# Values of two pairs turned by DMA, the first pair's weights doubled across the partitions, its context loaded from ScalarE's queue, and the last output in halves

## What is computed

```python
def _autocorrelation(Q, K, V):          # H = 8 heads, C = 2, L = 64
    ...
    corr = jnp.fft.ifft(qf * jnp.conj(kf), axis=2).real
    topk = int(C * np.log(L))           # 8
    w, idx = jax.lax.top_k(corr.transpose(0, 1, 3, 2), topk)
    w = jax.nn.softmax(w, axis=-1)
    for i in range(topk):
        g = jnp.minimum(idx[:, :, None, :, i] + pos, L - 1)
        out = out + w[:, :, None, :, i] * jnp.take_along_axis(v, g, axis=2)
...
x = x + jnp.tanh(g_xattn[0]) * _L0_xattn_ref(_layernorm(x, axis=-1), ctx_4096, ctx_4096)
x = x + jnp.tanh(g_ffn[0]) * _L0_ffn_ref(_layernorm(x, axis=-1), L0_ffn_W_gate, L0_ffn_W_up, L0_ffn_W_down)
```

## Time and profile before

| | |
|---|---|
| median of 3 runs | 218.98 us (218.32 to 219.37) |
| the profiled execution's time | 218.67 us |
| its span | 216.6 us |
| PE busy | 206.4 us, 95% of the span |
| ACT busy | 145.1 us, 67% |
| DVE busy | 135.2 us, 62% |
| POOL busy | 133.2 us, 61% |
| `turn` on ACT | 28 copies, 29.5 us |
| SP's loads | x of pair 0 issued at 0.72 us, the last one from 10.59 to 13.80 |
| PE on the chain that ended last | 87% |

### The profile page before, as it was taken

The page is one execution under the profiler, slowest core; times in us unless marked ns, Lnnn a source line. Parts: engine busy times, 40 slices in busy tenths (PEclk is TensorE's granted clock), DMA queues, the critical chain, the costliest instruction groups (busy, mean ns, idle before and its releaser), DMA issues.

```text
span 216.6 us, 6596 instructions
## 1 busy us (share of the span) xinstructions
PE 206.4 (95%) x2686; PEld 147.4 (68%) x2686; DVE 135.2 (62%) x407; ACT 145.1 (67%) x225; POOL 133.2 (61%) x161
## 2 busy tenths in 40 slices
PE   7899969889899999999999999999999999999994
PEld 2355239756467956897489858885788668959951
DVE  2499995998785793687767953668664437403421
ACT  2679897979978979959745996789266534401420
POOL 1202489679968988877696976488545854520430
PEclk9999979999999999999999999999999999999999
DMA  5999971002200130032001401111015500321001
GB/s 166 301 441 415 399 262 28 3 5 51 39 14 20 33 97 3 3 98 51 2 3 23 77 3 22 30 24 27 2 27 60 163 3 0 27 73 51 3 0 48
DMA packets 20061, 16.77 MB, mean 77 GB/s; under 512 B 15936, under 2 KB 16448, under 8 KB 19648
## 3 DMA queue, kind: packets, MB, share of 16 engines
q1 hardware_dynamic: 20032, 16.36, 25.6%
HBM read 10.59 MB, written 2.10 MB: 59 GB/s over the span
## 4 chain that ended last, share of the span: by engine, by line
PE 87%; POOL 4%; DVE 3%; ACT 3%; issue 1%; DVEq 0%; ACTq 0%
PE psum L895 45%; PE psum L1067 22%; PE psum L878 6%; PE psum L1018 4%; PE psum L908 2%; PE psum L886 2%; PE psum L988 2%; ACT k_spec L647 1%; POOL mixed_lo L579 1%; POOL prod_lo L563 1%; ACT v_spec L639 1%; PE psum L1003 1%; POOL hid_lo L593 1%; PE psum L957 1%; PE psum L969 1%
## 5 line engine op out<-in xcount | busy, mean ns | idle before, releaser
L895 PE MATMUL psum<-xt_hi,wg 128*128 128x128 f16 (+1 forms) x504 | 55.0, 216 | 0.0
L895 PE MATMUL psum<-xt_lo,wg 128*128 128x128 f16 (+1 forms) x504 | 54.9, 215 | 0.0
L895 PE MATMUL psum<-xt_hi,wu 128*128 128x128 f16 (+1 forms) x504 | 53.9, 213 | 0.0
L895 PE MATMUL psum<-xt_lo,wu 128*128 128x128 f16 (+1 forms) x504 | 53.9, 213 | 0.0
L895 PEld LDWEIGHTS psum<-xt_hi,wg 128*128 128x128 f16 x504 | 46.0, 99 | 4.4 <-issue 2.5
L593 POOL TENSOR_TENSOR hid_lo<-hid,hid_hi 128x512 f16<-128x512 f32 (+2 forms) x32 | 33.0, 1038 | 24.5 <-ACT hid_hi L711 24.3
L895 PEld LDWEIGHTS psum<-xt_hi,wu 128*128 128x128 f16 x504 | 44.8, 98 | 4.1 <-issue 3.4
L895 PEld LDWEIGHTS psum<-xt_lo,wg 128*128 128x128 f16 x504 | 46.1, 99 | 0.6
L895 PEld LDWEIGHTS psum<-xt_lo,wu 128*128 128x128 f16 x504 | 45.1, 98 | 0.7
L704 ACT ACTIVATE act<-psum 128x512 f32<-128x512 f32 (+2 forms) x32 | 17.2, 537 | 39.1 <-PE psum L895 38.9
L1067 PE MATMUL psum<-wd,hid_hi 128*128 128x512 f16 x112 | 42.5, 379 | 0.0
(11 more groups left out here) (92 smaller groups left out, 345.8 us busy)
## 6 DMA issues: line engine op xcount, KB each, us to landing
out<-x_sb SPq DMA_DIRECT2D x8, 256.0 KB, 2.5
wg<-w_gate SPq DMA_DIRECT2D x1, 1792.0 KB, 9.3
wu<-w_up SPq DMA_DIRECT2D x1, 1792.0 KB, 13.1
wd<-w_down SPq DMA_DIRECT2D x1, 1792.0 KB, 18.0
x_sb<-x SPq DMA_DIRECT2D x4, 256.0 KB, 5.1
ctx_sb<-ctx SPq DMA_DIRECT2D x4, 256.0 KB, 5.1
ctx_sb<-ctx SPq DMA_DIRECT2D x1, 1024.0 KB, 20.0
x_sb<-x SPq DMA_DIRECT2D x1, 1024.0 KB, 22.2
```

Of the source, the lines that this page charges most:

```text
L895: last = nc.tensor.matmul(psum[:, bank, a * n:(a + 1) * n], w[:, k, m * P:(m + 1) * P], xt[:, e, k, tok], start=(k == 0 and part == 0), st ...
```

## The change

- `turn` of pairs 1 and 2 is no longer four ACT copies but four DMAs from SBUF to SBUF, issued by SP, with a semaphore for each of the two pairs.
- Pair 0's `scale` writes the weights twice, side by side (64 lags, then the same 64), so that the transpose `wt` gives them in both halves of the partitions; `wspec:0` then has two parts instead of four, each with the "even" and the "odd" matmul on different halves of the partitions. `mask:0` writes into `expo`, and `match:1` waits for both `wt:0`.
- The context of pair 0 is issued from ACT's own queue, as its first instruction, no longer by SP.
- The last pair's `down` and `out` and its store go in two halves of 256 columns, the second half into another bank.
- `WARM_UP` is ((8, 4), (10, 7)), and `ORDER` is written anew.

```diff
+MOVED = (1, 2)
+TURNS = ((0, 32), (32, 0), (64, 96), (96, 64))
...
-rstd1:2 turn:1 wspec:0 sub:0.1 prod:1 exp8:0.1 exp:0.1 wspec:0.1 prod:1.1 turn:1.1 mask:0.1 lags:1 total:0.1
...
+rstd1:2 exp8:0.1 exp:0.1 wspec:0 prod:1 prod:1.1 total:0.1 lags:1 mask:0.1 mix_prod:0 scale:0.1 max:1 wt:0.1
...
-WARM_UP = ((12, 4), (8, 7))
+WARM_UP = ((8, 4), (10, 7))
...
-    w_whole = sb("w_whole", [L, 2, D])
+    w_whole = sb("w_whole", [P, 2, D])
...
+    def halves(p):
+
+        return (slice(0, D // 2), slice(D // 2, D)) if p == PAIRS - 1 else (slice(0, D),)
+
+    def down_psum(p, h):
+
+        cols = halves(p)[h]
+        return psum[:, down_bank(p) if h == 0 else w_bank(p, 0, 1), 0:cols.stop - cols.start]
...
+    def twice(part):
+
+
+        return probs[:, :, :, :, :].rearrange("p e c b l -> p (e c b l)")\
+            .rearrange("p (c b u l) -> p c b u l", c=CH, b=2, u=2)[:, :, part, :, :]
...
-            load(ctx_sb, cv, 0, 1, ctx_loaded[0])
...
+                if step == "turn" and p in MOVED:
+                    sp.wait_ge(v_copied, copies(p))
+                    for to, first in TURNS:
+                        sp.dma_start(v_turned[to:to + 32, e, :, :], v_spec[first:first + 32, e, :, :])\
+                          .then_inc(v_moved[p], 16)
...
-                    sp.wait_ge(out_ready, p + 1)
-                    sp.dma_start(outv[:, p:p + 1, :], x_sb[:, p:p + 1, :]).then_inc(stored, 16)
-            sp.wait_ge(stored, 16 * PAIRS)
+                    for h, cols in enumerate(halves(p)):
+                        sp.wait_ge(out_ready, p + h + 1)
+                        sp.dma_start(outv[:, p:p + 1, cols], x_sb[:, p:p + 1, cols]).then_inc(stored, 16)
+            sp.wait_ge(stored, 16 * (PAIRS + 1))
...
+            act.dma_start(ctx_sb[:, 0, :], ctx[0:P, :]).then_inc(ctx_loaded[0], 16)
...
-                if step == "turn":
-                    to, first = ((0, 32), (32, 0), (64, 96), (96, 64))[n]
+                if step == "turn" and p not in MOVED:
+                    to, first = TURNS[n]
...
-                if step == "scale" and mine:
-                    w = lag_cols(probs, p, n)
+                if step == "scale" and p == 0:
+                    to = twice(n)
                     dve.wait_ge(inv_ready, nth("total", p, n))
                     dve.wait_ge(masked, nth("mask", p, n))
-                    nc.vector.tensor_tensor(w, w, lag_sums(inv_total, p, n).unsqueeze(2).broadcast_to(w.shape),
+                    nc.vector.tensor_tensor(to, lag_cols(expo, p, n).unsqueeze(2).broadcast_to(to.shape),
+                                            lag_sums(inv_total, p, n).unsqueeze(2).unsqueeze(3).broadcast_to(to.shape),
                                             ALU.mult).then_inc(split_sems["scale", True], 1)
...
-                    b, m = n // 2, n % 2
-                    pe.wait_ge(w_high, nth("w_hi", p, b))
-                    if m == 0:
-                        pe.wait_ge(v_copied, b + 1)
-                    else:
-                        pe.wait_ge(prod_done, b + 1)
-                    nc.tensor.matmul(psum[:, w_bank(p, m, b), :], consts32[0:L, forward32(("even", "odd")[m])],
-                                     w_whole[:, b, :], start=True, stop=True).then_inc(w_spectra, 1)
+                    pe.wait_ge(w_high, nth("w_hi", p, n))
+                    pe.wait_ge(v_copied, n + 1)
+                    pe.wait_ge(prod_done, n + 1)
+                    for m, name in enumerate(("even", "odd")):
+                        last = nc.tensor.matmul(psum[:, w_bank(p, m, n), :], consts32[rows(m), forward32(name)],
+                                                w_whole[rows(m), n, :], start=True, stop=True)
+                    last.then_inc(w_spectra, 1)
...
+                    for h, cols in enumerate(halves(p)):
+                        for m in range(*span):
+                            for part, hid in enumerate((hid_hi, hid_lo)):
+                                last = nc.tensor.matmul(down_psum(p, h), hid[:, e, m, :], wd[:, m, cols],
+                                                        start=(m == 0 and part == 0),
+                                                        stop=(m == MT - 1 and part == 1))
+                        if n == STEPS - 1:
+                            last.then_inc(down_done, 1)
```

More of the change, by code:

```diff
@@ L221 @@
[L221 to L223 removed]
+warm:0 stats1:0 rstd1:0 kspec:0 q_norm:0 kcopy:0 qspec:0 kcopy:0.1 vspec:0 prod:0 stats1:1 lags:0 vcopy:0
+vcopy:0.1 prod:0.1 rstd1:1 kspec:1 max:0 lags:0.1 warm:0.1 sub:0 kcopy:1 match:0 exp:0 sub8:0 max:0.1 exp8:0
+vcopy:1 total:0 sub:0.1 q_norm:1 mask:0 sub8:0.1 scale:0 kcopy:1.1 stats1:2 wt:0 qspec:1 w_hi:0 match:0.1
@@ new lines @@
+h_lo:1.2 down:1.1 sub:4 turn:4.1 mix_prod:3.2 m_lo:3 match:4 exp:4 gate:2 m_hi:3.2 m_lo:3.1 mask:4 down:1.2
+tanh:2 exp8:4 h_hi:1.3 total:4 mix_prod:3.3 q_hi:5 h_lo:1.3 kspec:5 q_hi:6 silu:2 scale:4 down:1.3 kcopy:5
+up:2 m_lo:3.2 out:1 w_rows_hi:4 m_hi:3.3 w_t:4 w_rows_lo:4 kcopy:5.1 gate:2.1 hid:2 m_lo:3.3 h_hi:2 q_lo:5
+mix:3 tanh:2.1 w_t:4.1 mix:3.1 vcopy:5 silu:2.1 mix:3.2 k_lo:6 up:2.1 residual:3 turn:4.2 h_lo:2 turn:4.3
+qspec:5 rstd2:3 wspec:4 prod:5 gate:2.2 prod:5.1 p_hi:5 hid:2.1 p_hi:5.1 p_lo:5 mix_prod:4 up:2.2 tanh:2.2
```

145 lines of the change are left out of this document (67 added, 78 removed).

## The result

The kernel after takes **218.89 us** (median of 20 runs, 218.55 to 220.11), the kernel before 218.29 (20 runs, 217.06 to 219.39): ratio 1.0046, 95% interval 1.0027 to 1.0065. That is 0.6 us more where 2.35 us less were forecast, and above the range. The profiled execution took 219.05, its span is 217.0 us (before 218.67 and 216.6).

A forecast was written before the change was run, and what follows sets the result against it. PE's amount of work was taken as the bound. Gains of 0.55 + 0.9 + 0.6 + 0.3 = 2.35 us from 218.67 gave 216.3, plus 0.3 to the median: 216.6 us, range 214.9 to 218.4.

The forecast's parts named there:

- `gate:0` 0.55 us earlier: Start-up: the first feed-forward matmul starts 0.3 to 0.8 us earlier, 0.55 taken, bounds 0 and 1.2.
- First product at 8.0: Start-up: DVE's first product starts at 8.0 us in place of 9.21, 1.2 us earlier.
- The cold start: Rival: PE still at the 1.2 GHz level after 8 warm-ups, costing 2.9 us, 219.5 in all; chance 0.07.
- The stretch of DVE: DVE's work from first product to `residual:0`: from 16.05 to 16.85 us or somewhat more.
- The three terms of my sum: DVE's stretch: 0.8 more for `stats1:1`, 0.5 more for `scale:0`, 0.5 less waiting for `lags:0`.
- the second rival: Start-up lead eaten, waits moved to POOL, clock falls again: 0.8 us gain at most, 218.2; chance 0.17.
- The clock, 0.6: PE's clock fall near 30 us costs 1.25 us; half its removal, 0.6, taken as gain, bounds 0 and 1.25.
- The moved turns cost nothing: Turns by DMA from SP land behind the last load, near 34 us, covered by over 9 us of room.
- The named rival: Turns hold SP behind a full queue, pair 1's transposes come late: 217.5 to 219.5 us; chance 0.07.
- PE's waits, gain 0.9: PE's waits from 40 to 57 us shrink from 2.54 to 1.65 us, bounds 0 and 2.5.
- the wait on `match`: PE's `kspec:3` waits 1.3 us on DVE's `match:2`; the new list puts that earlier, so it goes.
- The end, 0.3: After PE's last matmul: halved output and store gain 0.3 us, bounds -0.2 and 0.5.

The follow-up runs named there:

- e12: e5 with the DMA turns issued by SP only after the last load of x has landed; 216.70 us, ratio 0.9926.
- e3: The kernel after with 12 warm-up matmuls and pair 0's context issued by SP again; 218.94 us, ratio 1.0029.
- e1: The kernel after with 12 warm-up matmuls in place of 8, nothing else; 218.93 us, ratio 1.0049.
- e9: The kernel after with the turns of pairs 1 and 2 back on ACT; 220.23 us, ratio 1.0091.
- e13: The kernel after with the DMA turns issued only after the last load of x has landed; 219.32 us, ratio 1.0057.
- e2: The kernel after with pair 0's context issued by SP again, still 8 warm-up matmuls; 219.14 us, ratio 1.0032.
- e14: e3 with the DMA turns issued only after the last load of x has landed, no added matmuls; 219.02 us, ratio 1.0023.
- e5: e3 with twelve more matmuls on zeros where PE idles before `gate:0`; 218.03 us, ratio 0.9999.
- e8: The kernel before with only the turns of pairs 1 and 2 given to SP's queue as DMAs; 219.90 us, ratio 1.0093.
- e6: The kernel before with 11 more matmuls on zeros, ahead of `xt:0` and `gate:0`; 217.68 us, ratio 0.9983.
- e16: e12 with the last pair's output whole, as in the kernel before; 217.44 us, ratio 0.9949.
- e15: e12 with ACT's copy `w_hi:0.1` moved ahead of `exp8:1` and `k_hi:2`; 216.58 us, ratio 0.9926.
- e7: e5 with ACT's copy `w_hi:0.1` moved ahead of `exp8:1` and `k_hi:2`; 218.25 us, ratio 1.0003.

## Why the prediction was wrong, by its own steps

- **`gate:0` 0.55 us earlier: it was 2.2 us later. This step failed, in three parts.** *First product at 8.0:* measured 9.45, and 7.89 to 8.69 in the eight traces where 12 warm-ups and the context on SP were back (e12 7.97, e3 8.06), so the path was right and its two side conditions were not. x was late by 0.57, and by 0.8 in e1, e9 and e13, where I took 0.2 and bounded it at 0.6. The Trainium skill (Trainium Kernel Development and Optimization, Key Constraints) says that DMAs of several issuers interleave on the same engines and that several issuers save only the issue time. By that rule the edit brings nothing and costs something, and the trace agrees: 4.04 against 3.47. *The cold start* I gave 7%, with "PE is not left idle for long" against it; PE idled 0.59 and 1.18 us. Its price was 2.9 us; e9 against after puts it at 1.4 at `gate:0`. *The stretch of DVE:* I had 16.85 us from the first product to `residual:0`; at full clock (e12) it is 25.45 - 7.97 = 17.48, and `gate:0` 31.10, where it was before. The three terms of my sum hold in e12's rows (0.82, 0.52, -0.54). What I put at nothing is new waits of DVE on PE (0.21 longer at pair 1's products, 0.07 at `max:1`, 0.21 before `residual:0`) and two `scales`, 0.2, which had stood in the wait that went. The whole lead of the start is eaten even when all goes well: the second rival's term, and it was no matter of chance. By my own terms, too, 25.26 to 25.0 was 0.26 and not 0.55.
- **The clock, 0.6:** at `gate:0` it paid 1.16, nearly all, in the profiled execution, and that was luck: there the fall stood at 7.5 us instead. I wrote one coin for one place. There were two places, and no trace has a fall at both: after and e13 fell at the start and not around `gate:0`; the other traces of the new order without added matmuls (e1, e2, e3, e9, e14) fell around `gate:0` and not at the start, e9 with no edit of the start at all. The kernel before keeps its clock in 49 of 125 runs, the kernel after in none of 20; by the groups that alone is some 0.6 us (0.4 of a fall of 1.6).
- **The moved turns cost nothing: they cost 1.3 us once start and clock are mended (e5 against e12).** In the old order it is 1.7 by the medians and 1.1 at equal clock (e8), some 0.6 of it by `scale:0.1` and not by the queue. In after itself nothing was won by issuing them late (e13), covered by the late `gate:0`. The named rival was close (SP behind a full queue) but put the damage at the transposes. The damage in e5 is PE's standing still in `up:0`. I had cited a rule for "land right behind the last load": the Trainium skill (DMA: Bandwidth & Descriptors, Queues, rings and completion order) has descriptors consumed in ring order on each DMA engine, and says too that completion is not first in, first out for an issuer. The trace bears out the second half: in e8 the first turn, issued at 15.64, had landed after 17.2 us, at 32.8, and the load issued at 10.65 only after 23.5, at 34.15. That part of the working was nearly right in time; what it left out is everything else that needs the DMA engines meanwhile.
- **PE's waits, gain 0.9:** the wait on `match` went, as worked out. From `gate:0` to the last matmul it is 180.6 us in after and e12, against 182.3 - 1.16 = 181.1 before, and 181.35 in e6: 0.5 to 0.7. POOL was waited for less than feared (0.4 on `mixed_lo`), but a new 0.9 on `residual:1` came. Mechanism right, size 0.2 to 0.4 too large.
- **The end, 0.3:** 0.2 in the profile of after, 0.5 in e12 against e16. Right.
- **The sum:** -2.2 + 1.2 + 0.5 + 0.2 = -0.3 by rounded terms (the two executions differ by 0.38) instead of +2.35. The first term alone missed by 2.8 us; the other three came to 1.9 where 1.8 were forecast, with the clock 0.6 above its term and the waits 0.4 below. The last step, 0.3 from the profiled execution to the median, rested on three runs; over 20 the median before is 218.29, 0.4 below that execution.

The best kernel, e12 (e15 is the same within its interval), is 0.74% faster than before, 1.6 us by that ratio. By the groups above 0.5 of it is the change's own work (216.7 against 217.20 at a clock of 1.00), and the rest is that it lost the clock in none of its runs.

**Still open:** whether PE waited for its instructions in `up:0` in e5 and e7, as the two packets suggest; no edit was made to test it. Why the fall is short in one run and long in the next, and where it stood in the runs of after that were not profiled, is open too. The price of the doubled weights alone (`scale:0` is 0.69 in place of 0.43, twice) was not run.

## What to carry to other kernels

Before giving work to the DMA engines, look at what is still queued: a transfer that is "free" because it is needed late can delay something that is needed sooner (here a load and, it seems, PE's instructions), and the remedy may be one wait that holds it back. Where the clock can fall at several places, group the runs by their mean clock before comparing anything, and count a repair as real only when no later gap gives it back. The listed clock does not show a slow start, so read there what one matmul takes. And before a difference between two traces is put down to an edit, look whether it stands in front of the edit's first effect: e9's 1.4 us did. A lead won ahead of an engine that is busy throughout is no lead: add up that engine's work to the next point where another engine is bound.
